# The 64-channel mix: four 64x64 matmuls in place of two with block-diagonal weights, and another order of the mixed image in DRAM

## What is computed

```python
q = x.reshape(b, c, h * w)
att = jnp.einsum('bcn,bdn->bcd', q, q)
rev = jnp.max(att, axis=-1, keepdims=True) - att
att_sm = jax.nn.softmax(rev, axis=-1)
res = jnp.einsum('bcd,bdn->bcn', att_sm, q)
x = gamma * res.reshape(b, c, h, w) + x
```

## Time and profile before

| | us |
|---|---|
| median of 3 runs | 6691.49 (6686.42 to 6696.54) |
| the profiled execution, its own time | 6684.96 |
| its span in the trace, first to last instruction | 6683.2 |
| TensorE busy with matmuls | 6293.8 (94% of the span) |
| TensorE busy with weight loads (beside matmuls) | 5492.5 (82%) |
| VectorE / ScalarE / GpSimd busy | 4013.7 / 3907.3 / 2554.8 |
| mean granted TensorE clock | 0.976 |

### The profile page before, as it was taken

One profiled execution on the slowest core, in us unless ns is written; L12 is line 12 of the kernel. 1 busy time (PEld: TensorE's weight loads), 2 busy tenths in 40 slices (PEclk: granted clock), 3 DMA queues, 4 the chain that ended last, 5 costly groups with the idle time before them and its releaser, 6 DMA issues.

```text
span 6683.2 us, 142217 instructions
## 1 busy us (share of the span) xinstructions
PE 6293.8 (94%) x37984; PEld 5492.5 (82%) x37984; DVE 4013.7 (60%) x7165; ACT 3907.3 (58%) x7001; POOL 2554.8 (38%) x2436
## 2 busy tenths in 40 slices
PE   6798799999999999999999999999999999999689
PEld 4495599788988899888998889978898889989579
DVE  1142377556775577655776467755676558866866
ACT  1233466555665566655665556655566557755865
POOL 0000255224552255423553235522455226632952
PEclk9898899999999999999999999999999999999999
DMA  6776655575656656476655756656565665534224
GB/s 193 227 214 213 201 187 186 181 223 178 186 178 201 206 183 187 156 239 189 186 185 171 238 173 186 186 183 218 178 186 177 202 202 168 168 120 140 80 83 129
DMA packets 770829, 1217.29 MB, mean 182 GB/s; under 512 B 78854, under 2 KB 475047, under 8 KB 770568
## 3 DMA queue, kind: packets, MB, share of 16 engines
q1 hardware_dynamic: 623112, 945.68, 48.1%
q10 hardware_dynamic: 147456, 268.50, 10.6%
HBM read 808.13 MB, written 405.73 MB: 182 GB/s over the span
## 4 chain that ended last, share of the span: by engine, by line
PE 89%; DMA 4%; ACT 2%; DVE 2%; issue 2%; POOL 1%; SPq 1%; ACTq 0%; DVEq 0%; POOLq 0%
PE ps L457 26%; PE ps L459 13%; PE ps L524 12%; PE ps L475 8%; PE ps L483 7%; PE ps L467 7%; PE ps L435 6%; PE ps L601 5%; DMA mixed<-x 3%; PE ps L535 3%; PE ps L649 1%; DMA pix<-in_x_pix 1%; ACT x L762 1%; DVE pix L1011 1%; DVE ps L1026 1%
## 5 line engine op out<-in xcount | busy, mean ns | idle before, releaser
L1045 POOL TENSOR_TENSOR mag<-mag,sgn 128x512 f32<-128x512 f32 x896 | 1041.5, 1162 | 2177.5 <-ACT mag L714 2151.7
L1060 POOL TENSOR_TENSOR split_a<-field,split_a 128x512 fp32r<-128x512 f32 x512 | 652.0, 1274 | 1798.8 <-ACT split_a L774 1798.8
L457 PE MATMUL ps<-tab_a,img 128*128 128x256 f32 x4096 | 1234.0, 383 | 6.9 <-issue 6.2
L457 PE MATMUL ps<-tab_b,mid 128*128 128x256 f32 x4096 | 1223.3, 380 | 0.4 <-DVE x L940 0.4
L905 DVE TENSOR_TENSOR held<-ps,v_t 128x512 f32<-128x512 f32 x896 | 619.7, 692 | 650.8 <-PE ps L524 609.6
L459 PEld LDWEIGHTS ps<-tab_a,img 128*128 128x128 f32 x4096 | 785.4, 192 | 109.6
L459 PEld LDWEIGHTS ps<-tab_b,mid 128*128 128x128 f32 x4096 | 778.2, 190 | 105.1
L459 PE MATMUL ps<-tab_a,img 128*128 128x128 f32 x4096 | 791.9, 275 | 0.0
L459 PE MATMUL ps<-tab_b,mid 128*128 128x128 f32 x4096 | 786.8, 274 | 0.0
L457 PEld LDWEIGHTS ps<-tab_a,img 128*128 128x128 f32 x4096 | 705.6, 193 | 83.0 <-issue 7.4
L475 PE MATMUL ps<-s_inv,split_a 128*128 128x256 f32 x4096 | 710.0, 317 | 66.5 <-POOL split_a L1060 37.7
(11 more groups left out here) (98 smaller groups left out, 11131.1 us busy)
## 6 DMA issues: line engine op xcount, KB each, us to landing
pix<-in_x_pix SPq DMA_DIRECT2D x256, 512.0 KB, 3.9
mixed<-x ACTq DMA_DIRECT2D x512, 256.0 KB, 3.1
img<-mixed SPq DMA_DIRECT2D x512, 256.0 KB, 2.7
tab_a<-filt SPq DMA_DIRECT2D x1024, 128.0 KB, 2.8
tab_b<-filt SPq DMA_DIRECT2D x1024, 128.0 KB, 2.8
coef<-res ACTq DMA_DIRECT2D x512, 256.0 KB, 2.0
out<-res SPq DMA_DIRECT2D x512, 256.0 KB, 3.2
pix<-in_x_rows SPq DMA_DIRECT2D x128, 512.0 KB, 4.8
```

Of the source, the lines that this page charges most:

```text
L457: nc.tensor.matmul(o_ps, src[:, 0, H * half:H * half + H], tab[:, N - 1::-1], start=True, stop=False)
L1045: nc.gpsimd.tensor_tensor(mag[:, a], mag[:, a], sgn[:, a], ALU.mult).then_inc(c_mult, 1)
L1060: nc.gpsimd.tensor_tensor(split_a[:, 1], src, split_a[:, 0].bitcast(F32), ALU.subtract)\
```

## The change

The mix takes the two units of a chunk together. Four matmuls of 64x64 weights by 64x512 data take the place of two of 128x128 by 128x512: the chunk's upper and lower 64 partitions (s) each meet the plain 64x64 matrix, once for each half of the columns. The output of half 0 goes to PSUM partitions 0 to 63, of half 1 to 64 to 127; s chooses the bank. All four are issued at the slot of the even unit, behind waits for the chunk, the weights and the copies of both units before. `mix_w` is now 128x64 (the matrix twice, one above the other), with no zeros to set. Steps with j%3 of 0 and 2 get four matmuls each, those with 1 none. ScalarE's copies and stores keep their slots; the store goes to another place in `mixed`, whose shape is now (4, 64, 32, 512), and `load_img` gathers a channel by 128 rows of 2 KB.

```diff
-        mixed = nc.dram_tensor("mixed", (C, H, 2 * N), F32, kind="Internal").ap()
+        mixed = nc.dram_tensor("mixed", (4, C, H // 4, 2 * N), F32, kind="Internal").ap()
-        mix_w = sb("mix_w", [128, 2 * C])
+        mix_w = sb("mix_w", [128, C])
...
             def load_img(c, d):
-                src = mixed[bass.ds(c, 1), :, :].rearrange("o p n -> p (o n)")
+                of_c = mixed[:, bass.ds(c, 1), :, :]
+                per_c = H // 4 * 2 * N
+                src = bass.AP(of_c.tensor, of_c.offset, [[2 * N, H // 4], [C * per_c, 4], [1, 2 * N]])
...
-                    def mix_one(m):
-                        e = 64 * g + 16 * r + m
-                        chunk = m // 2
+                    def mix_four(chunk):
+                        pe.wait_ge(xrows_in[chunk % 4], 16 * (8 * g + 2 * r + chunk // 4) + 16)
+                        pe.wait_ge(mix_w_ready, g + 1)
+                        pe.wait_ge(mix_copied, 64 * g + 16 * r + 2 * chunk + CR)
+                        pe.nop(nofuse=True)
+                        for half in range(2):
+                            for s in range(2):
+                                mm = nc.tensor.matmul(ps[C * half:C * half + C, 6 + s, :], mix_w[C * s:C * s + C, :],
+                                                      xrows[chunk % 4][C * s:C * s + C, 512 * half:512 * half + 512],
+                                                      start=True, stop=True)
+                                if half:
+                                    mm.then_inc(mix_mm, 1)
+
+                    for m in slots:
                         if m % 2 == 0:
-                            pe.wait_ge(xrows_in[chunk % 4], 16 * (8 * g + 2 * r + chunk // 4) + 16)
-                        pe.wait_ge(mix_w_ready, g + 1)
-                        pe.wait_ge(mix_copied, e - 1 + CR)
-                        nc.tensor.matmul(ps[:, 6 + m % 2, :], mix_w[:, :],
-                                         xrows[chunk % 4][:, 512 * (m % 2):512 * (m % 2) + 512],
-                                         start=True, stop=True).then_inc(mix_mm, 1)
-
-                    for m in slots:
-                        mix_one(m)
+                            mix_four(m // 2)
...
-                        rows_of = mixed.rearrange("c (s t) n -> (c s) (t n)", s=2)
-                        act.dma_start(rows_of[:, bass.ds(512 * (16 * r + m), 512)], staged[:, m % 2])
+                        rows_of = mixed[2 * (m % 2):2 * (m % 2) + 2].rearrange("g c t n -> (g c) (t n)")
+                        act.dma_start(rows_of[:, bass.ds(512 * (8 * r + m // 2), 512)], staged[:, m % 2])
...
-            link(nc.vector.memset(mix_w[:], 0.0))
...
-                for s in range(2):
-                    dst = mix_w[C * s:C * s + C, :].rearrange("p (c s) -> p c s", s=2)[:, :, s]
-                    ins = nc.vector.tensor_copy(dst, ps[C * s:C * s + C, 6, 0:C])
-                ins.then_inc(mix_w_ready, 1)
+                nc.vector.tensor_copy(mix_w[:, :], ps[:, 6, 0:C]).then_inc(mix_w_ready, 1)
...
-              "x_rows": x.reshape(nb, C, N, 2, 2, C).transpose(0, 4, 1, 5, 3, 2).reshape(nb, 2 * C, CHUNKS, 4 * N),
+              "x_rows": x.reshape(nb, C, N, 2, CHUNKS, 2, 2).transpose(0, 5, 1, 4, 6, 3, 2)
+              .reshape(nb, 2 * C, CHUNKS, 4 * N),
```

More of the change, by code:

```diff
@@ L766, in mix_store @@
                         act.nop(nofuse=True)
-                        rows_of = mixed.rearrange("c (s t) n -> (c s) (t n)", s=2)
-                        act.dma_start(rows_of[:, bass.ds(512 * (16 * r + m), 512)], staged[:, m % 2])\
+                        rows_of = mixed[2 * (m % 2):2 * (m % 2) + 2].rearrange("g c t n -> (g c) (t n)")
+                        act.dma_start(rows_of[:, bass.ds(512 * (8 * r + m // 2), 512)], staged[:, m % 2])\
                             .then_inc(mixed_out[m % 2], 16)
```

## The result

The changed kernel takes 6628.72 us (median of 4 runs, 6620.81 to 6629.89) against 6688.95 for the kernel before: a ratio of 0.9907, 95% interval 0.9889 to 0.9924, so **60 us or 0.9% faster**. Five further runs beside the experiments gave 6622.44, ratio 0.9906 (0.9892 to 0.992). The prediction said 6880 and slower.

The account below looks back on a forecast made before the run. PE was taken to bound the kernel, with the mix 5% of its chain. Full stages +148 and bare stages +40 on 6684.96 us gave 6873; the runs' median, 6.5 higher, made it 6880, range 6560 to 6985.

Parts of the forecast that it names:

- the number of slots: Mix visit: eight passes begin in program order and take five 0.43 us slots, 2.15 us, 0.43 more than before; chance 42%.
- the first rival: Mix visits: all four quarters run side by side, 1.20 us a visit, -100 us, total 6590; chance 26%.
- The round trip: Mix visits: PE going into 64x64 quarters and back costs 0.34 to 0.45 us, uncovered in full stages; 0.34 taken.
- the case's own range: Total with five slots: 6840 (no loss in bare stages) to 6980 us (0.45 a round trip, cold bare stages).
- PE as the bound of the full stages: Six inverse stages with channel steps: PE busy 245.65 of 246 us, so mix changes reach the end one for one.
- the cover: Full stages: PE's longer step hides ScalarE's and GpSimd's later work; with a short visit, 0.3 us a step.
- The bare stages: First two inverse stages, which do only the mix: +40 us together, bounds 0 to 109.
- The ring: Bare stages: both banks taken together make a copy-and-mix cycle of 3.95 us a chunk at full clock, 5.8 at half.
- PE's part was spare: Bare stages before the change: PE mixes one bank while the other is copied, so its time is spare.
- The clock: Bare stages: mean granted clock of 0.8, meaning the half level for 0.4 of the time.
- The order in DRAM: Stores and loads of `mixed`: nothing in full stages; in bare stages landings could move either way, 24 us kept in range.

Follow-up runs that it names:

- 16 passes: Changed kernel with each mix matmul cut into two pieces of 256 columns, a quarter's two pieces next to each other in the program: 6642.96 us.
- two quarters: Changed kernel with both banks fed from partitions 0 to 63, so only two quarters of the array work, each issued twice in a row: 6883.87 us.
- the added trips: Changed kernel with one tiny 64x64 matmul added in the 16 steps without mix matmuls of each full inverse stage: 6652.04 us.
- the run with two stores: Changed kernel with the mixed image channel by channel in DRAM and each unit's store as two DMAs of 64 rows: 6891.68 us, ratio 1.0299.
- Bank by bank: Changed kernel with each bank's two quarters issued behind that bank's own copy, bank 6 first, then bank 7: 6611.94 us, ratio 0.989.

## Why the prediction was wrong

**The step that failed** is the number of slots: "If passes begin in program order, the second pass of matmul 1 waits for its first, and nothing behind it begins". The records show all four first passes within 20 ns, and the runs with 16 passes and with two quarters show it for four passes in a row per quarter too. A visit has 2 slots, not 5: eight passes take 1.02 us with the way in, where the prediction had 2.15 without it. Line 447's rows, on which the step leaned, hold matmuls of one quarter alone; they show that a quarter's own passes queue, and nothing of what is behind them. The chance of 26% stood with the first rival, and that one happened. The Trainium skill, "TensorE: Matmul & The Clock Gate", Part 3, says that matmuls on different tiles overlap, starting about 4 ns apart; this trace agrees on the overlap, and the starts are 7 ns apart here. Its sentence that matmuls start strictly in program order does not hold once several matmuls of a quarter are queued: in the run with 16 passes quarter 4's first matmul started before quarter 1's second, which the kernel issues first. No run here shows two passes of one quarter side by side.

**The round trip was right**: 0.34 to 0.45 forecast, 0.35 to 0.40 measured by the added trips. It decides over the size of the gain: 0.86 less 0.36 is 0.50 us a visit, 192 of them 96 us; the full stages gave 89. The first rival's 1.20 us a visit was measured as 1.22. (Of the sums one does not come out: 169 and 109 us on 6691.5 make 6970 for the top of the case's own range, not 6980.)

**PE as the bound of the full stages was right, as the only bound nearly so**: they gained 89 of the 96 us, and PE's waits for GpSimd's split_a grew by 9 us in all. The prediction had seen that: it called the waits hidden by PE's longer step, and put the cover at 0.3 us a step if the visit were short. It is short, and in some steps the cover is gone. The first rival, with "all else has slack", had no term for it. PE never waits there for ScalarE's copies of the mix. How thin the cover is for ScalarE itself was shown by the run with two stores: 0.8 us more of issue a unit costs 37 us a stage.

**The bare stages** were costed for five slots at +40 (0 to 109) and came to +17. The ring was right in kind: a visit stands in the chain. That PE's part was spare before held for the first stage and not wholly for the second, with 14% of its chain. The clock, taken as unchanged at 0.8, fell to 0.50, with 2 slots of passes a chunk in place of 4; that the number of slots alone does it is not so, since two quarters with 4 slots had 0.50 too. Bank by bank takes 1 to 3 us a stage off, and the chain that it leaves is mostly the stores' landings, somewhat longer than before the change. With a higher clock as well the first stage is back at 131 us and the second is not, so the clock's part is seen in one stage and not in the other, and how the 8 us divide stays open. The first rival had no term for these stages and none for the stretches behind: +17 and +17 by the profiles. With the 11 us that the full stages fell short of its 100, that is about what lies between its 6590 and the 6629 that came.

**The order in DRAM** was costed at nothing, and outside the mix stages it is worth about 2 us at most; in the bare stages it is not told apart from the rest. What the prediction missed is that a DMA's price hangs on the shape of its rows; the change kept the store's 128 rows merged and gave the load an outermost step of 32, and both stayed fast.

## What to carry to other kernels

Four 64x64 matmuls on four quarters cost the time of one, fp32 passes included, even when their passes stand in the program one behind the other; but each visit pays 0.35 to 0.40 us for going in and out of quarters among 128x128 work, so it pays once it saves more than that, about one fp32 pass of 512 columns, and the fewer visits the better. The shorter visit uses up the cover of what ran beside it: look for waits that were nothing before. Take the banks of such a group one by one where nothing else hides the copies. Look at a strided DMA's packets per issue (here 144 against 130) before trusting its place in DRAM with the blame.

## What the runs showed that was not expected

- A store of 128 rows of 2 KB landed after 10.6 us in place of 3.4 when its rows were written as 2 by 64 with strides that don't merge, with two rows in flight in place of some 16, and the 16.8 MB of a bare stage then took 350 us.
- The granted clock of the bare stages differed from kernel to kernel: about 0.8 before the change, 0.50 after it, 0.50 with two quarters at four slots a chunk, 0.67 with four quarters at four slots, and 0.85 with the same and the banks taken one by one. None of the numbers given here explains the five, and it was not pursued.
- Eight weight loads of 64 columns for four quarters are over in 0.21 us, side by side as the passes are.
